# Half of the second thought's odd weight pairs split before it starts, the other half in its first step with slots of their own

## The chip, the cores and the metric

The kernel runs on one core of one Trainium2 chip. The metric is the device time of one execution in microseconds (us), the median of several runs. One execution is recorded by the hardware profiler, and all rows below are from that one.

## The reference

Two sequences of 2048 tokens with 1024 features, all in f32. The input goes through a half-weighted FFN block, a windowed attention and the same FFN block again. Of the FFN only the gate product and the "thought" need weights:

```python
x_norm = layer_norm(x, in_gamma, in_beta)
thought = x_norm[:, -1, :] @ agg_w + agg_b            # last token of each sequence, 1024 x 1024
for _ in range(K_STEPS):                              # 4 steps
    t = layer_norm(thought, pn_gamma, pn_beta)
    t = gelu(t @ d1_w + d1_b)                         # 1024 x 4096
    thought = thought + (t @ d2_w + d2_b)             # 4096 x 1024
broadcast = (thought @ bc_w + bc_b)[:, None, :]
gate = sigmoid(x @ gate_w + gate_b)
out = layer_norm(x + gate * broadcast, out_gamma, out_beta)
...
x = x + 0.5 * ffn(_layernorm(x))
x = x + attention(_layernorm(x))                      # windows of 128, squared relu, then @ w_o
x = x + 0.5 * ffn(_layernorm(x))
```

The thought is a chain of products for two rows (the last token of each sequence) whose 4 steps each go through all 32 MB of d1_w and d2_w.

## The kernel before

One program, PLAN, is a list of pieces in one order; each engine walks the list and issues what is its own of each piece, so the list sets the order on every engine's queue. TensorE (PE), VectorE (DVE), ScalarE (ACT), GpSimd (POOL) and SyncE (SP, which issues every DMA) meet by semaphores alone. The big products are f16 products of values split into a high and a low half (three products for one f32 product).

**Stages.** First come the folding of weights and the gate products of the 32 token tiles (to about 763 us). Stage 2 is the attention, in 16 groups of two tiles: per group `prep` pieces on DVE and ACT make the normalised tokens, a transposing DMA (`group_turn`, L989) brings them into the group's place, and PE makes q, v, score and collect from them. Stage 3 is the second FFN's gate products (from about 1734 us). The tokens of groups 0 and 1 lie in the slots 4 to 7 of `thought_units`; those of later groups in `gate_arena`.

**The thought** is computed twice (thought 0 beside stage 1, thought 1 beside stage 2), a few matmuls at a time between the pieces of the big work. `with_thought` hands them out as beats by a share of PE's time. A weight tile is 128 x 1024 f32, 512 KB; two of them make a pair, and a pair of tiles is used by 16 small matmuls in one go. d1 and d2 have 32 pairs together. A pair is used in one of these ways (`how`):

- `whole`: loaded as f32 and used as it is (L1258).
- `keep`: loaded as f32 (L851) into one of the slots for loads; `t_high` rounds it to f16 on ACT (L1469) into a slot for splits; `t_low` makes the rest on DVE (L1851); PE uses both halves from there (`t_unit`, L1268); SP stores the halves to `parts_scratch` (L945). So two tiles cost 2 loads, 2 ACT and 2 DVE instructions and 2 stores.
- `pair`: the stored halves are loaded back (L851, `thought_units<-parts_scratch`) and used (`t_pair`, L1268).

Thought 0 keeps the even pairs in its step 1. Thought 1 loads the even pairs back in its first step and keeps the odd ones there, all 16 of them, 32 tiles. From its second step on every pair is loaded back.

**Slots.** `thought_units` has 8 slots of a tile: 0 to 3 for loads (FOR_LOADS), 4 to 7 for splits (FOR_SPLITS). In thought 1's first step the loads of both kinds take turns in slots 0 to 3, so that in effect slots 3 and 0 hold the two tiles of a `pair` and slots 1 and 2 the raw tiles of a `keep`. From the second step on loads use all eight.

SP issues a slot's next load behind the piece that leaves the slot free, after waiting that it is free (`fetch_unit`, `await_left`). `t_high` waits for the raw tile and for a free split slot. Every one of these waits holds up all that stands behind it on its engine's queue.

## Time and profile before

| | us |
|---|---|
| median of 3 runs | 2074.18 |
| lowest and highest | 2071.38, 2074.87 |
| the profiled execution | 2078.41 |
| its span from first to last instruction | 2077.2 |
| TensorE busy | 1988.2 (96%) |
| VectorE busy | 1207.6 (58%) |
| ScalarE busy | 679.7 (33%) |
| GpSimd busy | 162.0 (8%) |

A difference from the time before counts only where TensorE is made to wait less or more, or to run at another clock. The rows that say where it waits are in the section after the next.

### The profile page before, as it was taken

The numbers are of one execution on the slowest core, as the hardware profiler recorded it, in microseconds if no ns is written. First come the engines' busy times: TensorE is split into PE (matmuls) and PEld (weight loads), VectorE is DVE, ScalarE is ACT, GpSimd is POOL, SyncE is SP. The second block draws the span as 40 slices with busy tenths as digits, with TensorE's granted clock in tenths as the row PEclk, the third lists the DMA queues.
The fourth block names the chain that finished last, engine by engine and source line by source line (L and its number), as shares of the span: only waits on it lengthen the run. The fifth ranks groups of instructions, "written<-read, shape, count | busy, mean of one in ns | idle before, by whom it ended". The sixth has DMA issues, their size and how long they took to land.

```text
span 2077.2 us, 30589 instructions
## 1 busy us (share of the span) xinstructions
PE 1988.2 (96%) x12010; PEld 1048.1 (50%) x12010; DVE 1207.6 (58%) x2152; ACT 679.7 (33%) x947; POOL 162.0 (8%) x278
## 2 busy tenths in 40 slices
PE   8999988999899899999999999999999999999997
PEld 3334433344343457655566655566656564444443
DVE  2323676223444465567666655655556536888887
ACT  0478545213223322223333212121112213444443
POOL 0000000000000010011001000000000001111111
PEclk9999998999999999999999999999999999999999
DMA  9599986879899743359989999798998947555552
GB/s 364 201 350 412 379 309 233 335 261 379 323 399 389 280 136 102 102 175 314 325 290 331 319 317 296 279 365 300 297 305 281 348 171 193 152 152 153 153 154 78
DMA packets 275214, 555.78 MB, mean 268 GB/s; under 512 B 149040, under 2 KB 149248, under 8 KB 274688
## 3 DMA queue, kind: packets, MB, share of 16 engines
q1 hardware_dynamic: 275072, 553.83, 76.6%
q8 instruction: 96, 1.57, 0.3%
q14 instruction: 46, 0.38, 0.0%
HBM read 406.93 MB, written 113.26 MB: 250 GB/s over the span
## 4 chain that ended last, share of the span: by engine, by line
PE 43%; DMA 4%; DVE 4%; SPq 2%; ACT 1%; issue 1%; POOL 0%; ACTq 0%; DVEq 0%
PE product_banks L1068 38%; PE product_banks L1203 2%; PE thought_acc L1268 2%; DMA thought_units<-parts_scratch 2%; DMA arena<-in_x 1%; SPq L989 1%; SPq L851 1%; DVE thought_units L1851 1%; DVE bn_parts L1492 0%; DMA gate_arena<-arena 0%; DMA arena<-x_scratch 0%; ACT arena L1384 0%; DVE arena L1663 0%; DVE arena L1639 0%; ACT arena L1387 0%
## 5 line engine op out<-in xcount | busy, mean ns | idle before, releaser
L1068 PE MATMUL product_banks<-gate_arena,arena 128*128 128x512 f16 x1536 | 355.5, 387 | 0.0
L1068 PE MATMUL product_banks<-wide_a,thought_units 128*128 128x512 f16 x1536 | 331.7, 379 | 0.8 <-DVE arena L1703 0.8
L1068 PE MATMUL product_banks<-gate_arena,wide_a 128*128 128x256 f16 x2688 | 301.6, 273 | 2.2 <-DMA gate_arena<-arena 2.2
L1068 PE MATMUL product_banks<-wide_b,gate_arena 128*128 128x512 f16 x1344 | 297.5, 379 | 0.0
L1068 PEld LDWEIGHTS product_banks<-gate_arena,wide_a 128*128 128x128 f16 x2688 | 261.6, 98 | 49.2 <-issue 19.3
L1068 PEld LDWEIGHTS product_banks<-gate_arena,arena 128*128 128x128 f16 x1536 | 150.6, 100 | 197.3 <-issue 40.4
L1068 PEld LDWEIGHTS product_banks<-wide_a,thought_units 128*128 128x128 f16 x1536 | 150.2, 98 | 182.6 <-DVE arena L1703 1.6
L1068 PEld LDWEIGHTS product_banks<-wide_b,gate_arena 128*128 128x128 f16 x1344 | 129.3, 98 | 160.8 <-issue 12.2
L1492 DVE BATCH_NORM_STATS2 bn_parts<-arena 128x6 f32<-128x512 f32 x256 | 164.2, 683 | 4.2
L1915 POOL TENSOR_TENSOR token_stats<-stats,minus_half 128x1 f32<-128x1 f32 x96 | 63.7, 664 | 1001.5 <-DVE stats L1500 848.4
L1672 DVE SCALAR_TENSOR_TENSOR gate_arena<-product_banks,gate_arena 128x256 f16<-128x256 f32 x128 | 54.1, 422 | 148.2 <-ACT gate_arena L1399 146.0
L1517 DVE SCALAR_TENSOR_TENSOR arena<-product_banks,inverse_gate,arena 128x512 f32<-128x512 f32 x64 | 47.9, 749 | 140.7 <-PE product_banks L1068 129.5
L1100 PE MATMUL product_banks<-wide_a,wide_b 128*128 128x512 f32 x256 | 120.8, 621 | 6.0 <-DMA wide_a<-in_w_attn 6.0
L1203 PE MATMUL product_banks<-arena,key_weights 128*128 128x512 f32 x248 | 114.3, 606 | 9.5 <-issue 5.3
L1915 POOL TENSOR_TENSOR stats<-stats,minus_half 128x1 f32<-128x1 f32 x64 | 68.1, 1063 | 705.0 <-DVE stats L1500 420.8
L1376 ACT ACTIVATE arena<-arena,token_stats 128x1024 f32<-128x1024 f32 x32 | 39.6, 1236 | 228.1 <-DMA arena<-in_x 228.0
L1405 ACT ACTIVATE arena<-product_banks,inverse_vo 128x512 f32<-128x512 f32 x64 | 43.8, 686 | 214.1 <-PE product_banks L1068 214.1
L1399 ACT ACTIVATE gate_arena<-product_banks 128x256 f16<-128x256 f32 x128 | 41.2, 379 | 199.8 <-PE product_banks L1068 199.8
L1268 PE MATMUL thought_acc<-thought_units,thought_parts 128*6 128x512 f16 x1344 | 96.8, 382 | 4.1 <-DMA thought_units<-parts_scratch 3.2
L1433 ACT ACTIVATE arena<-arena 128x512 f32<-128x512 f32 x64 | 40.3, 630 | 176.2 <-DVE arena L1517 176.2
L1663 DVE SCALAR_TENSOR_TENSOR arena<-arena 128x1024 f16<-128x1024 f32 x32 | 39.2, 1224 | 91.8 <-ACT arena L1387 91.8
L1100 PEld LDWEIGHTS product_banks<-wide_a,wide_b 128*128 128x128 f32 x256 | 48.5, 198 | 67.6 <-issue 67.5
(206 smaller groups left out, 2310.9 us busy)
## 6 DMA issues: line engine op xcount, KB each, us to landing
thought_units<-parts_scratch SPq DMA_DIRECT2D x272, 512.0 KB, 6.9
thought_units<-in_d_w SPq DMA_DIRECT2D x171, 512.0 KB, 7.5
arena<-in_x SPq DMA_DIRECT2D x64, 512.0 KB, 9.3
parts_scratch<-thought_units SPq DMA_DIRECT2D x64, 512.0 KB, 5.4
x_scratch<-arena SPq DMA_DIRECT2D x64, 512.0 KB, 8.2
thought_row<-in_d_w SPq DMA_DIRECT2D x53, 512.0 KB, 6.9
arena<-x_scratch SPq DMA_DIRECT2D x40, 512.0 KB, 7.5
gate_scratch<-arena SPq DMA_DIRECT2D x32, 512.0 KB, 8.0
```

The source lines that it names most:

```text
L1068: mm = pe.matmul(bank, left(i, k), right(j, k), start=(n == 0), stop=(n == 3 * KD - 1))
L1100: mm = pe.matmul(bank_ap(key), wide_b[:, e, d * P:(d + 1) * P], wide_a[:, e, h * BANK:(h + 1) * BANK], start=(e == 0), stop=(e == KD - 1))
L1203: mm = pe.matmul(bank_ap(key), weights_of(u)[:, side, :], value_slot(other)[:, h * BANK:(h + 1) * BANK], start=(side == 0), stop=(side == ...
L1268: mm = pe.matmul(thought_acc[at:at + PARTS * B, :], value, unit[:, part, h * BANK:(h + 1) * BANK], start=first and part == 0, stop=last an ...
L1376: act.activation(ph_slots[u % PREP_RING], px_slots[u % PREP_RING], ACT.Identity, bias=st[:, 1:2], scale=st[:, 0:1]).then_inc(h0_made, 1)
L1399: act.activation(queries[:, query_place(n * GROUP + i), 0, e - 1:e + 1, :], made[:, i], ACT.Copy, scale=QUERY_SCALE).then_inc(q_high_made, 1)
L1405: act.activation(value_slot(n * GROUP + i)[:, h * BANK:(h + 1) * BANK], bank_ap(key), ACT.Copy, scale=inverse["vo"][:, :]).then_inc(out_of ...
L1433: act.activation(res, res, ACT.Sigmoid).then_inc(gated_3, 1)
L1492: dve.bn_stats(bn_parts[:, h, :], source[:, h * BANK:(h + 1) * BANK]).then_inc(own.up(), 1)
L1517: dve.scalar_tensor_tensor(out=res[:, cols], in0=bank_ap(key), scalar=inverse["gate"][:, :], in1=bias[:, cols], op0=ALU.mult, op1=ALU.add) ...
L1672: low = dve.scalar_tensor_tensor(out=q[:, 1], in0=made[:, i], scalar=QUERY_SCALE, in1=q[:, 0], op0=ALU.mult, op1=ALU.subtract)
L1915: return pool.tensor_tensor(to, st[:, 2:3], minus_half[:, 0:1], ALU.pow)
```

## The change

16 of the 32 tiles that thought 1 kept in its first step (the pairs whose number is 1 modulo 4) are now loaded, rounded, split and stored between the two thoughts, from the last four gate tiles into group 2 of the attention. Slots 0 and 1 take their raw tiles, slots 2 and 3 the halves. In thought 1's first step these 8 pairs are loaded back as `pair`, so that the step has 24 pairs that are loaded back and 8 that are kept. The raw tiles of the kept ones get slots 6 and 7, their halves 4 and 5, and the `pair` tiles have all of 0 to 3. The first kept raw tiles wait for group 1's tokens to be used, their first halves for group 0's. Their `t_high` and `t_low` are placed only when a `t_unit` is one of the next two products of the thought. The wait of ACT for a score product is gone (it is now part of `await_left`).

```diff
     def use_of(self, owner):
 
         kind, n = owner
+        if kind == "tokens" or kind == "split" and self.splits[n].unit is None:
+            return "again"
...
         else:
-            slots = FOR_LOADS + (FOR_SPLITS if step else [])
+            slots = FOR_LOADS + FOR_SPLITS if step else FOR_SPLITS[GROUP:] if how == "keep" else FOR_LOADS
...
-        return "keep" if step == 0 and pair % 2 else "pair"
+        return "keep" if step == 0 and pair % 4 == 3 else "pair"
+
+    def split_between(self):
+
+        pairs = [("d1", [(k, c), (k, c + 1)]) for c in range(0, COLS_1, 2) for k in range(1, KD, 4)]
+        pairs += [("d2", [(k, 0), (k + 1, 0)]) for k in range(2, KH, 8)]
+        self.between = []
+        for matrix, pair in pairs:
+            made = []
+            for k, c in pair:
+                at = len(self.splits)
+                load = self.load(None, None, matrix, k, c, "keep", at, FOR_LOADS[:2])
+                slot = FOR_LOADS[2 + at % 2]
+                self.splits.append(Split(load, None, slot, self.take(slot, ("split", at))))
+                made.append(at)
+            for kind in ("high", "low"):
+                for at in made:
+                    self.between.append(self.step(None, (kind, at)))
...
-                        slot = FOR_SPLITS[at % len(FOR_SPLITS)]
+                        slot = FOR_SPLITS[at % (GROUP if tau else len(FOR_SPLITS))]
...
-            elif todo and i > first and s[0] in weights:
+            elif todo and i > first and s[0] in weights and (
+                    tau == 0 or any(x[0] == "unit" for x in [x for x in raw[i + 1:] if x[0] in weights][:2])):
...
-    out += paced([p for n in range(TILES - LATE, TILES) for p in plan_gate(n)], prep, 1.15, PE_PIECES)
-    out += [("sigmoid", TILES - 1, 1), ("gate_store", TILES - 1)]
-    out.append(("score_scale",))
-    out += plan_stage_2(0, B)
+    between = paced([p for n in range(TILES - LATE, TILES) for p in plan_gate(n)], prep, 1.15, PE_PIECES)
+    between += [("sigmoid", TILES - 1, 1), ("gate_store", TILES - 1)]
+    between.append(("score_scale",))
+    between += plan_stage_2(0, B)
+    out += paced(between, THOUGHTS.between, 0.38, PE_PIECES)
...
-        if kind == "split":
-            eng.wait_ge(unit_used, SPLITS[n].unit + 1)
+        if kind == "tokens":
+
+            eng.wait_ge(product_full, BANK_AT[("v", n, GROUP - 1, HALVES - 1)] + 1)
+        elif kind == "split":
+            if SPLITS[n].unit is not None:
+                eng.wait_ge(unit_used, SPLITS[n].unit + 1)
...
-                if n == STORE_2 or n == STORE_2 + GROUP:
-
-                    act.wait_ge(product_full, BANK_AT[("score", (n - STORE_2) // GROUP, 0)] + 1)
```

Line numbers shift by up to 38. **VectorE in the last gate tiles.** In the kernel before, L1626 is the first `prep` instruction of the attention's first tile (gate times thought), and the second L1492 of the piece belongs to the moments of the last gate tile:

```order
L1633 TENSOR_TENSOR arena<-arena,half_beta 128x1024
L1517 SCALAR_TENSOR_TENSOR arena<-product_banks,inverse_gate,arena 128x512 x2
L1626 TENSOR_TENSOR arena<-arena,thought_row 128x1024
L1509 SCALAR_TENSOR_TENSOR arena<-turn_banks,arena 128x512 x2
L1639 TENSOR_TENSOR arena<-arena 128x1024
L1492 BN_STATS bn_parts<-arena 128x6 x2
L1494 BN_AGGR stats<-bn_parts 128x2
L1500 TENSOR_SCALAR stats<-stats 128x1
L1492 BN_STATS bn_parts<-arena 128x6 x2
```

In the changed kernel L1886 is `t_low`, L1661 and L1527 are the two lines before:

```order
L1668 TENSOR_TENSOR arena<-arena,half_beta 128x1024
L1552 SCALAR_TENSOR_TENSOR arena<-product_banks,inverse_gate,arena 128x512 x2
L1886 SCALAR_TENSOR_TENSOR thought_units<-thought_units,unit_scale 128x1024
L1661 TENSOR_TENSOR arena<-arena,thought_row 128x1024
L1544 SCALAR_TENSOR_TENSOR arena<-turn_banks,arena 128x512 x2
L1674 TENSOR_TENSOR arena<-arena 128x1024
L1527 BN_STATS bn_parts<-arena 128x6 x2
L1529 BN_AGGR stats<-bn_parts 128x2
L1535 TENSOR_SCALAR stats<-stats 128x1
L1527 BN_STATS bn_parts<-arena 128x6 x2
```

One `t_low` now stands ahead of both.

**VectorE in group 1 of the attention.** Here nothing of the thought stood before. Now (L1683 to L1698 are `prep` of a tile, its last row ahead of the transposing DMA is L1698, and L1725 makes the weights that `collect` waits for):

```order
L1886 SCALAR_TENSOR_TENSOR thought_units<-thought_units,unit_scale 128x1024
L1668 TENSOR_TENSOR arena<-arena,half_beta 128x1024
L1674 TENSOR_TENSOR arena<-arena 128x1024
L1527 BN_STATS bn_parts<-arena 128x6 x2
L1529 BN_AGGR stats<-bn_parts 128x2
L1535 TENSOR_SCALAR stats<-stats 128x1
L1886 SCALAR_TENSOR_TENSOR thought_units<-thought_units,unit_scale 128x1024
L1683 SCALAR_TENSOR_TENSOR arena<-arena,stats,half_gamma 128x1024
L1688 SCALAR_TENSOR_TENSOR arena<-arena,stats 128x1024
```

Two `t_low` stand inside the chain of the group's second tile; a third stands ahead of the first tile's L1683.

**SyncE in thought 1's first step.** Before, for two neighbouring products of the thought (L945 stores halves, L972 to L976 fetch tokens, L995 and L1017 store tokens):

```order
L989 DMA_TRANSPOSE gate_arena<-arena 128x16x128
L851 DMA thought_units<-parts_scratch 128x1024 x2
L945 DMA parts_scratch<-thought_units 128x1024
L851 DMA thought_units<-in_d_w 128x1024
L945 DMA parts_scratch<-thought_units 128x1024
L851 DMA thought_units<-in_d_w 128x1024
L972 DMA arena<-in_x 128x1024
L976 DMA arena<-gate_scratch 128x1024
L972 DMA arena<-in_x 128x1024
L976 DMA arena<-gate_scratch 128x1024
L1017 DMA x_scratch<-arena 128x1024 x2
L851 DMA thought_units<-parts_scratch 128x1024 x2
```

Now (L983 stores halves, L889 loads, L1010 to L1055 are tokens):

```order
L889 DMA thought_units<-parts_scratch 128x1024 x4
L983 DMA parts_scratch<-thought_units 128x1024
L889 DMA thought_units<-in_d_w 128x1024
L983 DMA parts_scratch<-thought_units 128x1024
L889 DMA thought_units<-in_d_w 128x1024
L1010 DMA arena<-in_x 128x1024
L1014 DMA arena<-gate_scratch 128x1024
L1010 DMA arena<-in_x 128x1024
L1014 DMA arena<-gate_scratch 128x1024
L1055 DMA x_scratch<-arena 128x1024 x2
L889 DMA thought_units<-parts_scratch 128x1024 x6
```

Loads of stored halves come in fours and sixes, where they came in twos, and stores and raw loads are half as many.

## Rows read from the trace of the kernel before

**Rows 1.** Busy time of each engine by stretch; the first row is the columns.

```profile
core 0: us, PE busy (x) PEld busy (x) DVE busy (x) ACT busy (x) POOL busy (x), PEclk, DMA share, GB/s
718.00:918.00 200.00, 194.50 (x1279) 121.81 (x1278) 123.56 (x225) 52.77 (x76) 17.03 (x34) 1.00 0.40 126
918.00:1196.00 278.00, 266.52 (x1902) 168.22 (x1901) 194.58 (x356) 87.21 (x114) 24.86 (x46) 0.99 0.92 312
1196.00:1664.00 468.00, 462.13 (x3416) 281.97 (x3416) 270.94 (x552) 94.26 (x143) 32.22 (x78) 1.00 0.91 310
```

**Rows 2.** The same view in stretches of 52 us; PEclk is the granted clock.

```profile
936.00:988.00 52.00, 49.81 (x328) 28.42 (x326) 39.42 (x59) 20.53 (x26) 5.48 (x6) 0.97 0.98 314
988.00:1040.00 52.00, 49.74 (x368) 31.13 (x367) 34.44 (x58) 16.57 (x23) 4.05 (x10) 0.97 0.90 325
```

**Rows 3.** What TensorE waited for from 918 to 1196 us; total, times, longest.

```profile
PE product_banks L1203 <- issue: 3.3, 3, 2.0
PE thought_acc L1268 <- DMA thought_units<-parts_scratch: 2.5, 2, 2.3
PE product_banks L1068 <- DMA gate_arena<-arena: 2.2, 1, 2.2
PE thought_turn L1276 <- DVE t_wide L1858: 1.4, 1, 1.4
PE product_banks L1203 <- DVE key_weights L1690: 1.1, 1, 1.1
PE thought_acc L1268 <- DVE thought_units L1851: 0.9, 1, 0.9
```

**Rows 4.** Order of time, 960 to 1016 us: start, us, engine, line, idle before.

```profile
974.17 1.04 PE L1268 MATMUL thought_acc<-thought_units,thought_parts 128*6 128x512 f16 x16 [0.21 <-DMA thought_units<-parts_scratch]
...
992.58 1.51 SPq L851 DMA_DIRECT2D thought_units<-parts_scratch  x2
995.21 1.15 ACT L1469 ACTIVATE thought_units<-thought_units,unit_scale 128x1024 f16<-128x1024 f32 x1 [12.98 <-DMA thought_units<-in_d_w]
...
1007.78 1.79 PE L1268 MATMUL thought_acc<-thought_units,thought_parts 128*6 128x512 f16 x16 [2.26 <-DMA thought_units<-parts_scratch]
```

**Rows 5.** Instructions of L1469, 918 to 1196 us, and what they waited for.

```profile
L1469 ACT ACTIVATE thought_units<-thought_units,unit_scale x32: 1134/1148/1166, 918.6 to 1146.5; 128x1024 f16<-128x1024 f32 x32
...
  DMA thought_units<-in_d_w: 26.0, 8
```

**Rows 6.** Instructions of L1851, 918 to 1196 us.

```profile
L1851 DVE SCALAR_TENSOR_TENSOR thought_units<-thought_units,unit_scale x32: 1274/1280/1286, 927.4 to 1147.7; 128x1024 f16<-128x1024 f32 x32
```

**Rows 7.** What TensorE waited for from 718 to 918 us.

```profile
PE product_banks L1203 <- DVE key_weights L1690: 1.9, 1, 1.9
...
PE turn_banks L1077 <- ACT arena L1351: 0.5, 1, 0.5
```

**Rows 8.** ScalarE in order of time, 708 to 742 us: the tile's normalising.

```profile
739.87 1.24 ACT L1351 ACTIVATE arena<-arena,token_stats 128x1024 f32<-128x1024 f32 x1 [8.30 <-POOL token_stats L1922]
```

**Rows 9.** The transposing DMAs of L989, 740 to 870 us, issue to landing.

```profile
DMA to landing us min/median/max: 4.3/4.4/4.5
```

**Rows 10.** The same DMAs, 910 to 1196 us.

```profile
DMA to landing us min/median/max: 4.3/7.7/10.5
```

**Rows 11.** Order of time, 744 to 800 us: a transpose and its product.

```profile
762.55 1.91 SPq L989 DMA_TRANSPOSE thought_units<-arena  x1
...
773.17 21.12 PE L1068 MATMUL product_banks<-thought_units,wide_a 128*128 128x256 f16 x192
```

**Rows 12.** Order of time, 798 to 884 us: two more such pairs.

```profile
809.06 1.32 SPq L989 DMA_TRANSPOSE thought_units<-arena  x1
...
814.04 21.12 PE L1068 MATMUL product_banks<-thought_units,wide_a 128*128 128x256 f16 x192
...
855.47 1.93 SPq L989 DMA_TRANSPOSE gate_arena<-arena  x1
...
864.44 10.64 PE L1068 MATMUL product_banks<-gate_arena,wide_a 128*128 128x256 f16 x96
```

45 lines of the change are left out of this document (27 added, 18 removed).

## The prediction

> **What bounds the kernel now.** I read the busy time by stretch first: TensorE (PE) is the engine to look at, and what matters is not its busy time but what it lacks. From 718 to 918 us it lacks 200 - 194.5 = 5.5 us, from 918 to 1196 us 278 - 266.5 = 11.5 us, from 1196 to 1664 us 468 - 462.1 = 5.9 us [rows 1]. The second stretch is thought 1's first step, the third its other steps, the first is where the moved work goes. The step with the splits is thus the poorest: 4.1 us lacking in 100, against 1.3 in 100 later. The same view in short stretches shows that PE also had a lower clock there, 0.97 of full speed in two stretches of 52 us [rows 2], which is 2 x 0.03 x 52 = 3.1 us of work. So 11.5 + 3.1 = 14.6 us are to be had at most in this step. The waits of PE tell what they are: 3.3 and 1.1 us ahead of collect (L1203), 2.5 us for loads of stored halves, 2.2 us for a transposing DMA, 1.4 us for a copy of the sums, 0.9 us for a `t_low` [rows 3]. PE's own work stays the same: every pair still takes one run of 16 matmuls, whether from the splits or loaded back.
>
> **What goes away in the first step.** If it waited at the rate of the later steps, 5.9 / 468 x 278 = 3.5 us would remain [rows 1], so 14.6 - 3.5 = 11.1 us are owed to the splits and to what comes with them. I take it in two parts.
>
> (a) The loads of stored halves. One was issued at 992.6 us and PE began with its tiles at 1007.8 us, having waited 2.26 us; that run of 16 matmuls took 1.79 us where the one at 974 us took 1.04 [rows 4], so the clock had fallen behind the wait, to the lower of its two levels (1.2 instead of 2.4 GHz). With four slots in place of two such a load is issued one product of the thought earlier. The 2.5 us of [rows 3] and the lower clock of that stretch, 1.6 us [rows 2], should go: 4.1 us. (b) The rest of the 11.1 us, 7.0 us, are late collects, one late transposing DMA, a late `t_low`, and the other stretch at a lower clock. Behind them is the length of DVE's and ACT's queues. DVE runs 32 `t_low` of 1.28 us there [rows 6], 41 us of its 195 us [rows 1], and ACT's 32 `t_high` [rows 5] stood still for raw tiles 8 times, 26.0 us in all, once 12.98 us [rows 4, 5], with all else on ACT behind them. Halving the number halves these, 3.5 us; the raw tiles are now fetched two products ahead, so it may be more, up to the whole 7.0, or, if it is the attention's own chain that is late, nothing. I take 3.5. Sum: 4.1 + 3.5 = 7.6 us less, between 0 (nothing of it depends on the splits) and 11.1.
>
> The Trainium skill speaks for more than the first term: in "TensorE: Matmul & The Clock Gate", section "HAM oscillation — how this bites in real kernels", each wait of PE that throttles it is paid a second time in slow matmuls. The wait at 1007.8 us agrees (1.79 us for 1.04). Taken for every wait it would make the gain larger, and no row here shows that: of the 11.5 us of waits the clock's share is 3.1.
>
> **What comes between the thoughts.** 16 `t_high` of 1.15 us on ACT and 16 `t_low` of 1.28 us on DVE [rows 5, 6] go where ACT is busy 53 and DVE 124 of 200 us [rows 1]: 18 and 20.5 us, for which there is room on both. The loads and stores, 32 of 0.5 MB, are 17 MB in some 150 us, 112 GB/s on top of 126 GB/s, where 312 GB/s are moved later [rows 1]. So none becomes a bound. What costs is a `t_low` or a block of DMAs inside a chain that PE waits for. I find three such places.
>
> - The last gate tile. PE already waits 0.5 us there for the normalised tile [rows 7], which ACT makes at 739.9 us after a chain over DVE and POOL [rows 8]. A `t_low` stands in DVE's queue ahead of that chain, where DVE runs without a gap: 1.28 us more. It would be nothing if DVE had a gap, and I see none there; two more in the worst case 2.6.
> - Group 1's tokens. The second transposing DMA of group 1 is issued at 809.1 us and takes 4.4 us [rows 9], so it lands at 813.5; PE begins with them at 814.0 [rows 12]. The slack is 0.5 us, but it stands behind a wait for collect of 1.9 us [rows 7] that would take up part of a delay. Now a store and a load of 0.5 MB each are issued just ahead of it. With 4.4 us to landing as before it costs nothing; with the 7.7 us of the loaded stretch [rows 10] 3.3 - 0.5 = 2.8 us. I take 1.
> - Group 2's tokens. The DMA is issued at 855.5 us, lands at 859.9, and PE needs it at 864.4 [rows 12], slack 4.5 us. Three `t_low` in DVE's chain move it by 3 x 1.28 = 3.8 us: it fits by 0.7 us. With 7.7 us to landing it is late by 2.6. I take 1.
>
> For group 0's last tokens the DMA is issued at 762.6 us and PE comes at 773.2 [rows 11]: slack 10.6 - 4.4 = 6.2 us, against four `t_low` at most, 5.1 us. Nothing. The first kept raw tiles of thought 1 wait for group 1's value products, which lie before the collect that thought 1 has to wait for anyway. Nothing either. SP holds up the token DMAs behind a `t_low` by a microsecond or two, at places where their data are needed some 10 us later. Sum: 1.3 + 1 + 1 = 3.3 us more, between 0 and 8.
>
> **The sum.** -7.6 + 3.3 = -4.3 us. The profiled execution took 2078.4 us of which its span is 2077.2, and lies 4.2 us above the median; 2078.4 - 4.3 = 2074.1 there, 2074.2 - 4.3 = 2069.9 us for the median. Later steps of thought 1 have the same loads in a slightly different order, and stage 3 is untouched: both weigh nothing in the sum.
>
> **The rivals.**
>
> *Slower.* The transposing DMAs land later. They take 4.3 to 4.5 us in the quiet stretch [rows 9], and 7.7 (median) to 10.5 us [rows 10] where stores and loads of the thought go beside them; the change brings such stores and loads into the quiet stretch. At 7.7 us the prices are 1.3 at the gate tile, 5.1 + 3.3 - 6.2 = 2.2 for group 0, 2.8 and 2.6 us for groups 1 and 2: 8.9 us, and if the clock falls behind three of the waits as in [rows 4], 0.75 us in a run and as much again in the next, 1.5 us each, 4.5 more. If of the first step only (a) is won, 4.1 us, this gives 13.4 - 4.1 = 9.3 us slower, 2083.5 us; with the full 7.6 us won 2080.0. I take 2080. It decides from about 5.5 us to landing on. Against it: the traffic stays under what the loaded stretch has, 238 against 312 GB/s. Chance 0.14. The Trainium skill has the mechanism ("DMA: Bandwidth & Descriptors", "Queues, rings and completion order"): all that SP issues goes through one row of rings, and each engine consumes the descriptors in ring order, so a transpose stands behind the store and load issued ahead of it. With the same page's some 358 GB/s for a core, two tiles ahead would be an estimated 2.9 us; the rows' own difference is 3.3 us.
>
> *The waits only move.* The waits in the first step come from how the pieces of attention and thought happen to meet, each 1 to 2 us and none of them twice at the same place. Then a new order of beats makes new ones at the rate of before, and only (a) and a little of (b) is won, say 5, while 3.3 are paid: 2072.5 us. For it: half of the splits still stand there, the step gets denser (its first to last product in less time), and DMA is 0.92 busy in the step [rows 1], so that even with more slots a load may come late. Chance 0.30.
>
> *More is won.* If ACT's standing still for raw tiles is what makes the collects and the transposing DMA late, all of (b) goes: -11.1 + 3.3 = -7.8, and with 1.3 alone paid between -9.8: 2065.5 us. Chance 0.14.
>
> *It does not do what it says* can be left out: the rows of the order show the splits moved and the number of stores halved in the step.
>
> **How the numbers follow.** The forecast of 2069.9 us has 0.42, from 2067 to 2072.5. The range of 8 in 10 reaches from 2063.5 to 2078.5: it takes in the larger gain, the moved waits, and a third of the slower case. A difference of 0.2% is 4.15 us, about what a measurement of this kernel can tell from no change, so faster means under 2070.0 us. That is the case in 0.14 of the larger gain, about 0.25 of the 0.42 of the forecast, and 0.06 of the moved waits: 0.45. Slower means over 2078.3: 0.12 of the first rival and 0.02 of others: 0.14. The same: 0.41.
>
> **What would show it.** In the changed kernel's busy time by stretch PE should lack about 11.5 - 5.5 = 6 us in the first step, and the granted clock should be 1.00 in all but perhaps one stretch; the waits for `parts_scratch` in it should be under 0.5 us; ACT's waits for raw tiles (L1504 there) under 10 us. From 718 to 918 us PE should lack about 5.5 + 3.3 = 9 us, with 1.8 us at the last gate tile. The transposing DMAs there should take 4.4 to 5.5 us. Wrong would be: over 12 us lacking between the thoughts, or the first step at 10 us still, with collects waiting for DVE as before.

## The result, and the profile after

| | before | after |
|---|---|---|
| time, us (median, range, runs) | 2074.52 (2071.38 to 2077.39, 4) | 2102.51 (2100.13 to 2103.86, 4) |
| ratio to before | | 1.0123, interval 1.0103 to 1.0143 |
| span of the profiled execution, us | 2077.2 | 2101.5 |
| granted clock over the span | 0.986 | 0.981 |

The change makes the kernel 1.2% slower: 25.5 us (21 to 30) by the ratio, 28 by the medians. The forecast was 4.3 us faster, and its range ended at 2078.5.

Where the time went is told by the same piece of work in both traces. What stood at 718 us before stands at 720 now, what stood at 918 at 933, 1196 at 1217, 1664 at 1688. So 13 us were lost between the thoughts, 6 in the first step of thought 1, 3 in its later steps. Stage 3 keeps the distance. The 2 us at 718 are older than the change: up to there the kernels run all but the same program, and the single profiles of all the kernels below lie between 4 us ahead of before and 3 us behind it at that place. The cuts follow the attention's pieces; the thought's own first step ends inside the second stretch, at 1156 us before and at 1148 now (the copy of its last sums, L1858 and L1893). First the busy time by stretch, cut at these places (before: [rows 1]):

```profile
core 0: us, PE busy (x) PEld busy (x) DVE busy (x) ACT busy (x) POOL busy (x), PEclk, DMA share, GB/s
720.00:933.00 213.00, 196.89 (x1286) 122.94 (x1284) 142.72 (x243) 69.44 (x92) 19.79 (x34) 0.98 0.63 205
933.00:1217.00 284.00, 269.39 (x1944) 169.13 (x1941) 172.16 (x334) 70.00 (x98) 21.15 (x46) 0.98 0.85 290
```

Between the thoughts TensorE lacks 213 - 196.9 = 16.1 us (5.5 before), at a clock of 0.98. In the first step it lacks 284 - 269.4 = 14.6 (11.5 before), at 0.98 as well (0.99 before). What it waited for in the first step (columns: total, times, longest; before: [rows 3]):

```profile
PE thought_acc L1306 <- DMA thought_units<-parts_scratch: 12.0, 4, 6.5
PE thought_turn L1276 <- DVE thought L1926: 2.1, 1, 2.1
PE product_banks L1106 <- DMA gate_arena<-arena: 0.5, 1, 0.5
```

All that stood in the rows of before but the loads is nearly gone: late collects, the late transposing DMA, the copy of the sums and the late `t_low` made 8.9 us of waits, and now 2.6 are left. The loads of stored halves made 2.5 us, and now make 12.0. ScalarE's 16 `t_high` of the step waited 0.7 us for raw tiles, where 32 had waited 26.0 [rows 5]:

```profile
L1504 ACT ACTIVATE thought_units<-thought_units,unit_scale x16: 1132/1145/1151, 947.1 to 1121.5; 128x1024 f16<-128x1024 f32 x16
...
  DMA thought_units<-in_d_w: 0.7, 1
```

The longest of the load waits, TensorE in order of time (start, duration, ..., times; in brackets the idle time before it):

```profile
1065.27 1.04 PE L1306 MATMUL thought_acc<-thought_units,thought_parts 128*6 128x512 f16 x16
...
1074.21 0.60 PE L1306 MATMUL thought_acc<-thought_units,thought_parts 128*6 128x512 f16 x8
1081.34 1.02 PE L1306 MATMUL thought_acc<-thought_units,thought_parts 128*6 128x512 f16 x8 [6.53 <-DMA thought_units<-parts_scratch]
```

A beat with two pairs ran at 1065.3 us, the next one began at 1074.2 and stood still in its middle for 6.53 us. SyncE's queue around it, and the time from issue to landing of the two loads (L889) that are issued at 1065.9 and 1066.3 us:

```profile
1060.35 1.09 SPq L1010 DMA_DIRECT2D arena<-in_x  x1
...
1063.66 0.99 SPq L1055 DMA_DIRECT2D x_scratch<-arena  x2
```

```profile
L889 SPq DMA_DIRECT2D thought_units<-parts_scratch x2: 320/391/462, 1065.9 to 1066.3; - x2
...
DMA to landing us min/median/max: 14.0/14.4/14.9
```

They were issued as soon as the first beat had freed its slots, and landed 14.0 and 14.9 us later. Ahead of them stand ten transfers of 0.5 MB that SyncE had issued from 1058.2 us on and that were still on their way: two stores of halves, two raw tiles, four token fetches (two each of L1010 and L1014) and two token stores. Meanwhile the DMA engines moved 417 GB/s, more than the 290 of the whole step:

```profile
1066.00:1081.00 15.00, 8.81 (x88) 7.06 (x80) 6.60 (x12) 4.51 (x7) 0.27 (x2) 0.88 1.03 417
```

At that rate a transfer of 0.5 MB takes 1.26 us, and the ten with the two loads themselves are twelve, an estimated 15.1 us: the landing time is that of a queue. The beats are 8.9 us apart. In the front part and in the prediction a count has to be put right here: a pair takes 8 matmuls, and the run of 16 is a beat of two pairs. It matters for the slots, below.

What TensorE waited for between the thoughts (before: [rows 7]):

```profile
PE product_banks L1241 <- DVE key_weights L1725: 6.1, 1, 6.1
PE product_banks L1106 <- DVE gate_arena L1707: 3.6, 1, 3.6
PE thought_turn L1270 <- DMA t_wide<-arena: 3.2, 1, 3.2
PE turn_banks L1115 <- ACT arena L1389: 1.6, 1, 1.6
```

The wait for the last gate tile is 1.6 us, where 1.8 was expected. The large ones were not: 3.6 us for the rounded queries of a product (L1707 on VectorE) and 6.1 us for the scores' weights (L1725), ahead of group 0's first collect; and 3.2 us for the rows with which thought 1 begins (`t_wide`), which SyncE now fetches at 882.0 us, behind the last stores of halves, and fetched at 865.9 us before.

### The profile page after: what moved, and what is told of

Same layout as the page of the kernel before. It is cut to its first block and busy times, and to the rows that moved or that the text cites. A ratio compares the mean times of both kernels' runs of the same rounds, so it can differ in the third digit from the quotient of the medians.

```text
span 2101.5 us, 30604 instructions
## 1 busy us (share of the span) xinstructions
PE 1992.9 (95%) x12010; PEld 1050.0 (50%) x12010; DVE 1207.6 (57%) x2152; ACT 679.1 (32%) x947; POOL 161.1 (8%) x278
## 5 line engine op out<-in xcount | busy, mean ns | idle before, releaser
L1527 DVE BATCH_NORM_STATS2 bn_parts<-arena 128x6 f32<-128x512 f32 x256 | 164.3, 684 | 4.4
L1707 DVE SCALAR_TENSOR_TENSOR gate_arena<-product_banks,gate_arena 128x256 f16<-128x256 f32 x128 | 54.1, 422 | 146.7 <-ACT gate_arena L1437 144.4
L1698 DVE SCALAR_TENSOR_TENSOR arena<-arena 128x1024 f16<-128x1024 f32 x32 | 39.2, 1224 | 109.0 <-ACT arena L1425 109.0
```

Of the source, the lines that this page charges most:

```text
L1527: dve.bn_stats(bn_parts[:, h, :], source[:, h * BANK:(h + 1) * BANK]).then_inc(own.up(), 1)
L1707: low = dve.scalar_tensor_tensor(out=q[:, 1], in0=made[:, i], scalar=QUERY_SCALE, in1=q[:, 0], op0=ALU.mult, op1=ALU.subtract)
```

## The experiments

Each kernel was timed against the kernel before. "Behind" is (ratio - 1) x 2077 us, with its interval. Single executions of one kernel differ by some us (2070 to 2080 in e6), so where one profile is read, differences under 3 us are not made use of. The distance between two kernels of the table is uncertain by 4 to 7 us, by their two intervals. e2, e3, e5, e6, e7b, e9, e10b and e17 use wrong weights or factors in place of what they leave out, and tell of time alone.

| kernel | ratio | interval | us behind before |
|---|---|---|---|
| the changed kernel | 1.0123 | 1.0103 to 1.0143 | 25.5 |
| e1 between alone | 1.0074 | 1.0052 to 1.0096 | 15.4 |
| e2 first step alone | 1.0018 | 1.0004 to 1.0032 | 3.7 |
| e3 no loads between | 1.0093 | 1.0073 to 1.0114 | 19.3 |
| e4 high, low in turn | 1.0079 | 1.0061 to 1.0097 | 16.4 |
| e5 first step all loaded, 8 slots | 0.9927 | 0.9911 to 0.9942 | -15.2 |
| e6 first step all loaded, 4 slots | 0.9987 | 0.9975 to 0.9999 | -2.7 |
| e7b no work between | 1.0047 | 1.0035 to 1.0060 | 9.8 |
| e8 clear of the scores | 1.0108 | 1.0093 to 1.0122 | 22.4 |
| e9 two more slots | 1.0034 | 1.0016 to 1.0052 | 7.1 |
| e10b VectorE's work alone | 1.0098 | 1.0077 to 1.0120 | 20.4 |
| e11 beats 3 us later | 1.0081 | 1.0057 to 1.0106 | 16.8 |
| e12 in VectorE's gaps | 1.0121 | 1.0098 to 1.0145 | 25.1 |
| e13 the same, raw tiles earlier | 1.0062 | 1.0044 to 1.0080 | 12.9 |
| e14 e13 and beats later | 1.0072 | 1.0057 to 1.0088 | 15.0 |
| e15 before, beats later | 1.0009 | 0.9994 to 1.0023 | 1.9 |
| e16 e13, last rounding behind the values | 1.0086 | 1.0064 to 1.0109 | 17.9 |
| e17 e16 and two more slots | 0.9999 | 0.9985 to 1.0013 | -0.2 |

### The two halves of the change apart

e1 keeps the sixteen splits between the thoughts and has the first step of before (the diffs here and below are against the changed kernel where nothing else is said):

```diff
-        return "keep" if step == 0 and pair % 4 == 3 else "pair"
+        return "keep" if step == 0 and pair % 2 else "pair"
...
-            slots = FOR_LOADS + FOR_SPLITS if step else FOR_SPLITS[GROUP:] if how == "keep" else FOR_LOADS
+            slots = FOR_LOADS + (FOR_SPLITS if step else [])
...
-                        slot = FOR_SPLITS[at % (GROUP if tau else len(FOR_SPLITS))]
+                        slot = FOR_SPLITS[at % len(FOR_SPLITS)]
...
```

> The kernel before with the sixteen extra splits between the thoughts and nothing else of the change: the eight pairs are rounded and stored there, and then once more in the first step as before, so the first step is that of before and the extra stored copies are read by nobody. Theory of the queue (the traces of before and after side by side): the loads, roundings and stores between the thoughts stand ahead of token fetches and transposing DMAs on SP's queue and ahead of the token tiles' instructions on ACT, which costs 13.6 us between 718 and 893 us; this kernel then takes 2074.5 + 13.6 = 2088 us (2084 to 2092). The prediction's own step (3.3 us between the thoughts) would give 2078. If it is 2074, the loss between the thoughts comes from somewhere else.

e2 leaves out all that stands between the thoughts:

```diff
-        self.split_between()
+        self.between = []
...
+for n, load in enumerate(LOADS):
+    if load.how == "pair" and (load.matrix, load.k, load.c) not in STORE_OF:
+        STORE_OF[load.matrix, load.k, load.c] = STORE_OF[load.matrix, load.k - (1 if load.matrix == "d1" else 2), load.c]
```

> The kernel after without anything between the thoughts: in the first step of the second thought, and in the later ones, the eight pairs that would have been stored between the thoughts load the stored halves of the pair before them (k-1, or k-2 in d2), so their products are computed from the wrong weights, with the same number of loads, matmuls and slots as in the changed kernel. The prediction's step (7.6 us won in the first step) gives 2067. Theory of the slots (the stored halves still come into four slots that a beat uses up two at a time, and there are half again as many of them): the first step loses 6 to 8 us by itself, 2081 (2078 to 2084). Rival, that the first step of the changed kernel only suffers from what happened between the thoughts: 2074 or less.

Measured: 15.4 us behind for e1 (10.8 to 20), 3.7 for e2 (0.8 to 6.6). The sum is 19.1, and 6.4 us of the changed kernel's 25.5 come only with both together; by the intervals that rest may also be nothing. The profiles speak for nothing: at 718 us, ahead of all that was changed, the changed kernel's stood 2.1 us behind before, e1's 0.6 and e2's 1.3 ahead, and counted from there their spans are 22.2, 14.8 and 6.4 us longer, which leaves 1.0. What e1 waited for between the thoughts, and then what e2 waited for in the first step:

```profile
PE product_banks L1240 <- DVE key_weights L1724: 3.4, 1, 3.4
PE product_banks L1105 <- DVE gate_arena L1706: 3.3, 1, 3.3
PE thought_turn L1269 <- DMA t_wide<-arena: 3.2, 1, 3.2
```

```profile
PE thought_acc L1310 <- DMA thought_units<-parts_scratch: 9.6, 4, 6.5
```

So most of the loss is made where the prediction had 3.3 us, and the first step wins nothing by itself where it had 7.6. The theory written before these runs was right on e1 and 3 us too dark on e2.

### What the price between the thoughts is made of

e3 takes the raw tiles away, e7b the work (it keeps loads, waits and stores), e10b ACT's part of the work.

```diff
-                load = self.load(None, None, matrix, k, c, "keep", at, FOR_LOADS[:2])
+                load = len(self.loads)
+                self.loads.append(Load(matrix, k, c, "resident", at, FOR_FIRST[at % 2], 0, None))
...
```

> The changed kernel with the sixteen roundings and stores between the thoughts, but without their sixteen loads of raw tiles: both halves are made from a tile that is already in the chip (the first thought's row), so the stored halves are wrong and ACT waits for no load there, and SP issues no load there; ScalarE's and VectorE's work and the stores stay. Theory of the queue: ACT's waits for the raw tiles (25.8 us in six waits) and SP's loads are what holds up the token tiles, so 9 to 12 of the 13.6 us go: 2092 (2089 to 2095). Rival, that the rounding work itself (16 x 1.15 us on ACT, 16 on DVE) and the stores cost it: 2100 to 2103.

```diff
...
+                to, of = parts_at(split.slot)[:, 0], unit_at(load.slot)
+                if split.unit is None:
+                    to, of = to[:, 0:8], of[:, 0:8]
+                act.activation(to, of, ACT.Copy,
...
+                if split.unit is None:
+                    low, raw, high = low[:, 0:8], raw[:, 0:8], high[:, 0:8]
...
```

> The changed kernel with its loads, waits and stores between the thoughts, but the roundings there done on 8 columns of 1024, which takes their work from ACT and DVE (the stored halves are wrong, and in the second thought the pairs concerned load the pair before instead). With the loads taken away the loss between the thoughts stayed at 10.5 of some 13 us. If the work is what costs, above all a rounding's second half on VectorE ahead of the scores' weights (collect waited 6.1 us), 7 to 10 us go here: 15 to 18 us behind the kernel before. If it is the waits and the queue that cost, nothing goes: 25 us behind.

```diff
...
+                if split.unit is None:
+                    to, of = to[:, 0:8], of[:, 0:8]
+                act.activation(to, of, ACT.Copy,
...
+                                         in1=parts_at(split.slot)[:, 0] if split.unit is not None else half_gamma[:, :],
```

> The changed kernel with ACT's half of the roundings between the thoughts done on 8 columns, and VectorE's half at full length (reading gamma instead of the first half; the stored halves are wrong, and the second thought loads the pair before instead). With both halves' work gone the kernel was 9.8 us behind before, with both there 25.5. If VectorE carries the price (it is busy 128 us of the 191 there, ACT 65), this stays at 22 to 25 us behind; if ACT's 18 us do, about 10; if each does a part, 15 to 18.

Measured: 19.3 us behind without the loads, 9.8 without the work, 20.4 with VectorE's work alone. Both theories of mine had a part wrong. The loads, which I held for the cause, are 6 us of it. The work is 15.7, more than I gave it, of which VectorE's 16 instructions of 1.28 us account for 10.6 and ACT's 16 of 1.15 for the other 5.1. The 6 and the 5.1 are no larger than what two such times can differ by; the 15.7 and the 10.6 are clear of it. Loads, work and the 3.7 of e2 add up to 25.6 of the 25.5. Both engines had been idle for a third of the stretch and more. Without the work TensorE waits between the thoughts as before (1.9 us for the weights), but for 1.9 us for the row of the thought:

```profile
PE product_banks L1246 <- DVE key_weights L1733: 1.9, 1, 1.9
PE thought_turn L1275 <- DMA t_wide<-arena: 1.9, 1, 1.9
```

How so little work costs so much is to be seen in the changed kernel's queues. VectorE ahead of the collect, in order of time:

```profile
815.03 0.29 DVE L1725 SCALAR_TENSOR_TENSOR key_weights<-key_weights 128x128 f32<-128x128 f32 x1
815.24 1.28 DVE L1886 SCALAR_TENSOR_TENSOR thought_units<-thought_units,unit_scale 128x1024 f16<-128x1024 f32 x1
818.94 1.23 DVE L1698 SCALAR_TENSOR_TENSOR arena<-arena 128x1024 f16<-128x1024 f32 x1 [2.43 <-ACT arena L1425]
820.09 0.34 DVE L1721 SCALAR_TENSOR_TENSOR key_weights<-product_banks,score_scale,keep_prev 128x128 f32<-128x128 f32 x1
```

Behind the first weights (815.03) come a `t_low` (L1886) and the `prep_low` of group 1's second tile (L1698), which waits for ACT, and only then the other weights (820.09). TensorE has been idle since 815.6:

```profile
806.25 4.12 PE L1106 MATMUL product_banks<-gate_arena,thought_units 128*128 128x128 f16 x48 [3.62 <-DVE gate_arena L1707]
...
821.68 5.29 PE L1241 MATMUL product_banks<-arena,key_weights 128*128 128x512 f32 x8 [6.12 <-DVE key_weights L1725]
```

In the kernel before it came to the same collect at 810.54, having waited 1.92 us:

```profile
810.54 3.67 PE L1203 MATMUL product_banks<-arena,key_weights 128*128 128x512 f32 x8 [1.92 <-DVE key_weights L1690]
```

The two rows of the collect also show the clock: its 8 matmuls took 5.29 us, where before 8 took 3.67, and over their first 3.6 us the granted clock was 0.55 (before 1.00). The wait of 6.1 us is paid again in part. That agrees with the Trainium skill, "TensorE: Matmul & The Clock Gate", section "HAM oscillation — how this bites in real kernels", which the prediction had cited and then counted only for waits of 2 us.

And why is VectorE late? Its token tiles are. SyncE's queue of the changed kernel, from the transposing DMA of group 0's second tile to group 1's first fetch (L1010):

```profile
771.22 2.06 SPq L1027 DMA_TRANSPOSE thought_units<-arena  x1
773.34 0.85 SPq L960 DMA_DIRECT2D gate_scratch<-arena  x1
774.24 0.44 SPq L983 DMA_DIRECT2D parts_scratch<-thought_units  x1
774.72 0.91 SPq L889 DMA_DIRECT2D thought_units<-in_d_w  x1
775.68 1.19 SPq L960 DMA_DIRECT2D gate_scratch<-arena  x1
776.98 0.40 SPq L1010 DMA_DIRECT2D arena<-in_x  x1
```

The fetch is issued at 776.98 us. Before, it was at 766.11:

```profile
766.11 0.85 SPq L972 DMA_DIRECT2D arena<-in_x  x1
```

Ahead of it in the queue stand two gate stores, a store of halves and a raw tile; the last two are new and account for 2.2 of the 10.9 us. The other 8.7 are those of the transposing DMA of group 0's second tile, which is issued at 771.2 us instead of 762.6 [rows 11]. VectorE and ScalarE ahead of it:

```profile
759.76 1.28 DVE L1886 SCALAR_TENSOR_TENSOR thought_units<-thought_units,unit_scale 128x1024 f16<-128x1024 f32 x1
760.96 1.28 DVE L1683 SCALAR_TENSOR_TENSOR arena<-arena,stats,half_gamma 128x1024 f32<-128x1024 f32 x1
...
762.31 1.15 ACT L1504 ACTIVATE thought_units<-thought_units,unit_scale 128x1024 f16<-128x1024 f32 x1 [4.69 <-DMA thought_units<-in_d_w]
766.19 0.63 ACT L1402 ACTIVATE arena<-arena 128x512 f32<-128x512 f32 x1 [2.73 <-DVE arena L1552]
```

And the tile's instruction (L1683 now, L1648 then) in the kernel before:

```profile
753.17 1.31 DVE L1648 SCALAR_TENSOR_TENSOR arena<-arena,stats,half_gamma 128x1024 f32<-128x1024 f32 x1
```

It starts 7.8 us later. Two of these are the older lateness of this profile; the others are four `t_low` (at 732.2, 740.5, 753.9 and 759.8 us) and a `t_high` (749.9), which stand one behind the other in the chain that leads to this tile, and move it by 1.1 to 1.3 us each. The long wait of ScalarE for a raw tile (4.69 us, until 762.31) cost nothing here: ScalarE stood idle behind it again until VectorE had made its next input, at 766.19.

So each queue in turn holds up the next: VectorE and ScalarE the token tile behind roundings, SyncE the next group's fetches behind that tile's transposing DMA, VectorE the weights behind that group's tiles. VectorE begins the first tile of group 1 at 785.3 us instead of 773.1, 12.2 us later, while TensorE, beside whose products for group 0 these tiles are made, begins them 3.2 us later (776.3 instead of 773.2 [rows 11]). So VectorE has 9 us less for the two tiles, with further `t_low` among their instructions. The experiments agree: the same fetch is issued at 770.7 us in e7b, without the work, and at 772.6 in e3, without the raw tiles.

### Can the order cure it?

e4 sets first and second halves in turn, e8 also keeps them from the stretch before the collect.

```diff
-            for kind in ("high", "low"):
-                for at in made:
+            for at in made:
+                for kind in ("high", "low"):
                     self.between.append(self.step(None, (kind, at)))
```

> The changed kernel with one edit: between the thoughts the pieces come as high, low, high, low instead of high, high, low, low, so that three pieces instead of two lie between the fetch of a raw tile and the rounding that waits for it, and a rounding's second half follows its first one piece later. Theory of the queue: ACT's waits for raw tiles shrink, and with them a third to a half of the 13.6 us: 2097 (2094 to 2100). Rival, that the roundings' work counts and not the waits: 2102.

```diff
-    out += paced(between, THOUGHTS.between, 0.38, PE_PIECES)
+    clear, other, due = (between.index(("q", 0, 3)), between.index(("collect", 0, 1))), list(THOUGHTS.between), 0.0
+    for i, piece in enumerate(between):
+        out.append(piece)
+        if piece[0] in PE_PIECES and not clear[0] <= i <= clear[1]:
+            due += 0.47
...
```

> The kernel with high, low, high, low between the thoughts (16.4 us behind the kernel before) with one more edit: no rounding stands between the fourth product of group 0 (q 0 3) and its first collect, where two second halves of 1.28 us stood on VectorE ahead of the scores' weights; the others come a little closer together (0.47 a piece instead of 0.38). If VectorE's order there is what makes the collect wait (6.15 us, against 1.92 before) and what lowers the clock behind it (0.89 in 800:830), 4 to 6 us go: 10 to 12 us behind the kernel before. If the wait comes from the token tiles' late start instead, nothing goes: 16.

Measured: e4 16.4 us behind, 9 less than the changed kernel, more than I had expected from it. e8 22.4: my reason for it fell. The wait for the weights became 5.2 us instead of 6.15, since the fetches of group 1 were still 6 us late, and a new one of 7.1 us came ahead of thought 1, whose row is fetched by SyncE behind the last store of the splits, which the edit had moved there.

e12, with the halves in turn as in e4, sets each piece by hand into a place where VectorE was idle in the trace of before, and group 1's fetches ahead of the stores.

```diff
...
+PLACES = [("gate", 28, 0, 0), ("gate", 28, 0, 2), ("gate", 28, 1, 0), ("gate", 28, 1, 2),
+          ("gate_store", 31), ("prep_fetch", 1), ("gate_store", 31), ("prep_fetch", 1),
+          ("q", 0, 1), ("q", 0, 4), ("score", 0, 0, 2), ("v", 0, 1, 1, 1), ("v", 0, 1, 1, 2), ("collect", 0, 1),
+          ("q", 1, 0), ("q", 1, 2), ("q", 1, 3), ("q", 1, 4), ("q", 1, 5), ("q", 1, 6), ("q", 1, 7), ("v", 1, 0, 0, 1),
+          ("v", 1, 1, 0, 1), ("score", 1, 1, 2), ("score", 1, 0, 0), ("score", 1, 0, 2),
+          ("v", 1, 1, 1, 0), ("v", 1, 1, 1, 1), ("v", 1, 1, 1, 1), ("v", 1, 1, 1, 2), ("v", 1, 1, 1, 2), ("collect", 1, 0)]
...
```

> The changed kernel with its sixteen roundings between the thoughts set by hand into the places where the trace of before shows VectorE idle (9.2 us while group 1's tokens come, 2 to 6 us around the collects and the q products of group 1), high and low in turn, group 1's token fetches ahead of the stores, and none in the last three gate tiles. If the price is that VectorE's and ACT's work stands ahead of the token tiles, most of it goes: collect's wait returns to 2 to 3 us (6.1), and the kernel is 8 to 12 us behind before instead of 25.5. If the sum of work counts wherever it stands: 16 or more.

Measured: 25.1 us behind, nothing won. TensorE's waits between the thoughts tell why:

```profile
PE product_banks L1258 <- ACT arena L1460: 12.1, 1, 12.1
...
PE product_banks L1258 <- DVE key_weights L1742: 1.9, 1, 1.9
```

Group 0's collect waited 1.9 us, as before: that far the places were right. Group 1's collect waited 12.1 us for values that ACT copies (L1460). SyncE, and ACT, around it:

```profile
862.71 1.94 SPq L1044 DMA_TRANSPOSE gate_arena<-arena  x1
...
865.74 0.44 SPq L906 DMA_DIRECT2D thought_units<-in_d_w  x1
```

```profile
872.36 1.15 ACT L1521 ACTIVATE thought_units<-thought_units,unit_scale 128x1024 f16<-128x1024 f32 x1 [7.67 <-DMA thought_units<-in_d_w]
873.41 0.67 ACT L1460 ACTIVATE arena<-product_banks,inverse_vo 128x512 f32<-128x512 f32 x1
```

The raw tile that was fetched at 865.74 us, behind a transposing DMA and a store, is the one for which ACT's rounding waited 7.67 us, until 872.36; the values stood behind that rounding. Work ahead of the tokens had been exchanged for a wait at the head of a queue. e13 fetches each raw tile earlier, by one more rounding in the gate tiles (its diff is against e12); e16 sets the last rounding behind the values (against e13).

```diff
-          ("gate_store", 31), ("prep_fetch", 1), ("gate_store", 31), ("prep_fetch", 1),
+          ("gate", 29, 0, 1), ("gate", 29, 0, 2), ("gate_store", 31), ("prep_fetch", 1),
+          ("gate_store", 31), ("prep_fetch", 1), ("q", 0, 1), ("q", 0, 4), ("score", 0, 0, 2), ("v", 0, 1, 1, 1),
...
```

> As the kernel whose roundings stand in VectorE's idle places, with one of them more in the gate tiles (behind gate 29 0 2), and by that every later one a place earlier, so that the fetch of each raw tile is issued 8 us or more ahead of its rounding. In the kernel before it group 0's collect waited 1.92 us, as before, but group 1's waited 12.1 us, because on ACT the rescaled values of that group stood behind a rounding that waited 7.7 us for its raw tile. Theory of the order (what counts is which token instruction stands behind a rounding or behind a load that a rounding waits for): that wait returns to 1.1 us and the kernel is 25.1 - 11 = 14 us behind before (11 to 17). Theory of the amount (64 us of DMA, 18 of ACT and 20 of VectorE cost their price wherever they stand): 20 to 25 us, with waits elsewhere.

```diff
-          ("v", 1, 1, 1, 0), ("v", 1, 1, 1, 2)]
+          ("v", 1, 1, 1, 2), ("collect", 1, 0)]
```

> As the kernel with the raw tiles earlier (12.9 us behind before), with one rounding moved: the last one's first half stands behind the values of group 1 on ACT (behind v 1 1 1 2) instead of ahead of them, where it waited for its raw tile and group 1's collect waited 5.2 us for it. Theory of the order: the collect waits 1.1 us as before, and with the lower clock behind it 4 to 6 us go: 7 to 9 us behind before. Theory of the amount: the wait turns up elsewhere, 11 or more.

Measured: 12.9 us behind (9 to 17) for e13 and 17.9 (13 to 23) for e16. TensorE's waits between the thoughts, of e13 and then of e16:

```profile
PE product_banks L1259 <- ACT arena L1461: 5.2, 1, 5.2
```

```profile
PE product_banks L1259 <- DVE key_weights L1743: 5.2, 2, 3.3
PE thought_turn L1288 <- DMA t_wide<-arena: 3.0, 1, 3.0
```

e13 came where the theory of the order had it: half of the 25.5 us depended on what stood behind what. e16 did not: the wait for the values went, and one for the weights (3.3 us) and one for the thought's row (3.0) came in its place; by their intervals its time can't be told from e13's. So the order explains about half, and I found none that makes the 16 splits free in these 175 us.

### The first step: slots

e5 and e6 load every pair of the first step back, and round nothing in thought 1 or between the thoughts. They differ in the slots alone: e5, whose diff this is, has eight and e6 four.

```diff
...
-        return "keep" if step == 0 and pair % 4 == 3 else "pair"
+        return "pair"
...
-            slots = FOR_LOADS + FOR_SPLITS if step else FOR_SPLITS[GROUP:] if how == "keep" else FOR_LOADS
+            slots = FOR_LOADS if matrix == "agg" else FOR_LOADS + FOR_SPLITS
...
```

> Nothing between the thoughts, and no rounding in the second thought at all: in its first step every pair loads stored halves, into eight slots as in the later steps (the pairs that no one stored load the halves of the pair before them, so their products are computed from wrong weights). This is the end to which the change goes a part of the way. If the rounding in the first step (64 us of ACT and DVE, 16 pairs) is what TensorE lacks there, all 14.6 us of lack and low clock of the first step shrink to the 3.5 of a later stretch of that length: 11 us faster than before. If the loads are the bound (twice as many as in the changed kernel's pairs that are loaded), it is no faster than before, within 3 us.

> As the one with eight slots, but the stored halves of the first step come into four slots, as in the changed kernel. Theory of the slots: a beat uses up two pairs, so with four slots their successors are fetched only one beat ahead (landing 3 to 15 us after issue, beats 5 to 16 us apart), and TensorE waits for them: 8 us or more behind the kernel with eight slots. Rival, that four slots are enough and the changed kernel's first step loses to its bursts of stores and raw loads: within 3 us of the eight slots.

Measured: 15.2 us faster than before with eight slots (12 to 18), 2.7 with four. First e5's stretch of the first step, in which TensorE lacks 1.5 us at full clock, then e6's wait for loads there:

```profile
918.00:1196.00 278.00, 276.49 (x2050) 175.03 (x2048) 164.83 (x343) 54.42 (x86) 19.60 (x47) 1.00 0.87 293
```

```profile
PE thought_acc L1310 <- DMA thought_units<-parts_scratch: 6.5, 6, 2.5
```

The idea of the change is thus right: with no rounding in the step the kernel can be 15 us faster, and 10 of them are what TensorE no longer lacks in the step (1.5 us for 11.5). But four slots take 12.5 of the 15 away again. e9 tries the same in the changed kernel, whose loads get the two slots of the first thought's row; the gates are multiplied by another vector in its place:

```diff
...
-            slots = FOR_LOADS + FOR_SPLITS if step else FOR_SPLITS[GROUP:] if how == "keep" else FOR_LOADS
+            slots = FOR_LOADS + FOR_SPLITS if step else FOR_SPLITS[GROUP:] if how == "keep" else FOR_LOADS if matrix == "agg" else FOR_LOADS + FOR_FIRST
...
-                dve.tensor_tensor(gb, gb, thought_row[:, GROUP_OF[u // GROUP][0], :], ALU.mult).then_inc(gate_spread, 1)
+                dve.tensor_tensor(gb, gb, half_gamma[:, :], ALU.mult).then_inc(gate_spread, 1)
```

> The changed kernel whose stored halves in the first step of the second thought come into six slots instead of four: the two slots under the first thought's row are taken for them, and the token tiles' gates of stage 2 are multiplied by gamma instead of that row (a wrong factor of the same size, the same instructions). With nothing rounded in the first step, eight slots against four were worth 12.4 us. Theory of the slots: TensorE's waits for stored halves in the first step (12.0 us in four waits) fall below 4, and the kernel gains 6 to 9 us on the changed one: 17 to 20 us behind before instead of 25.5. Rival, that the waits come from where single bursts of transfers happen to fall (6.5 us of them are one wait): less than 3 us gained.

Measured: 7.1 us behind, 18.4 less than the changed kernel. The first step by stretch and waits:

```profile
928.00:1200.00 272.00, 270.27 (x2002) 172.99 (x2000) 177.67 (x348) 69.64 (x98) 20.29 (x47) 1.00 0.88 306
```

```profile
PE thought_turn L1281 <- DVE thought L1931: 1.7, 1, 1.7
```

No wait for a load is left. The 12.0 us of waits and the clock, 0.98 to 1.00 over 284 us or 5.7 us, are together 17.7 of the 18.4; by the collects in both traces the work of those 284 us takes 266 in e9 (929 to 1195 us). Against e1, which has the same work between the thoughts and the first step of before, e9 is 15.4 - 7.1 = 8.3 us shorter (2 to 14): with six slots the changed first step is worth about what the prediction gave it with four, 7.6.

### Where the beats fall

Two long waits of the changed kernel hang on which piece a beat falls behind (the 6.5 us for a load, and 4.0 us at 1581.6 us for a copy of the sums that stands on VectorE behind a token instruction). e11 moves all beats of thought 1; e14 does so in e13, and e15 in the kernel before.

```diff
-def with_thought(main, beats):
+def with_thought(main, beats, due=0.0):
...
-    out += with_thought(plan_stage_2(B, GROUPS - 1), THOUGHTS.beats[1])
+    out += with_thought(plan_stage_2(B, GROUPS - 1), THOUGHTS.beats[1], -3.0)
```

> The changed kernel with every beat of the second thought set 3 us later among the main work, nothing else. Theory of accident: two of its longest waits in the second thought (6.5 us for stored halves whose loads were issued behind four token fetches and two stores, 4.0 us for the copy of the sums behind a token instruction that waits for its tile) hang on which piece a beat falls behind; moved by 3 us they vanish or change by 3 us or more in sum, so the time moves by 3 to 8 us, more likely down. Theory that these are the price of four slots and of the share of work: the same time within 2 us, with waits of like sum elsewhere.

> As the one with the raw tiles earlier, and with the second thought's beats 3 us later as well. In the changed kernel that shift alone took the time from 25.5 us behind before to 16.8. If the two causes add up (the order between the thoughts; where the beats of the second thought fall), this is 14 - 8 = 6 us behind before (2 to 10), and still not faster, since the first step keeps four slots. If the shift only bought back what the loss between the thoughts had displaced, it brings nothing here: 12 to 16 us behind.

> The kernel before with the second thought's beats 3 us later, nothing else: a control. If where the beats fall is a matter of accident of some 5 us in either kernel, this differs from before by 3 to 8 us in either direction. If only the changed kernel, with four slots for half again as many stored halves, depends on it, this is the time before within 2 us.

Measured: 16.8 us behind for e11, 8.7 less than the changed kernel; but 15.0 for e14, 2.1 more than e13, and 1.9 for e15, which can't be told from before. So the shift is no cure, and it doesn't add up with the order. In the profile of e11 the same two places did change (3.6 us of wait for the load instead of 6.5, and 7.4 for loads in all instead of 12.0; none at the sums), others came (3.8 us for other sums, 4.4 for squares). Why it won 8.7 us (2 to 15) in one kernel and nothing in the next I leave open.

### Both together

> That kernel with six instead of four slots for the stored halves of the first step (the token tiles' gates of stage 2 multiplied by gamma instead of the first thought's row, as in the earlier kernel with two more slots). There the slots took 18.5 us off the changed kernel. If order and slots are the two causes of the loss and add up, this is 8 - 18 = some 10 us faster than before (2062 to 2072 where before is 2077): the change's idea pays once both are cured. If part of the 18.5 us only made up for the loss between the thoughts (at 1130 us that kernel stood 3.8 us ahead of before, having been 11.5 behind at 870), the gain is 0 to 4 us.

e17 is e16 with the edit of e9. Measured: 0.9999, the time of before. Slots were worth 18.4 us in the changed kernel and 18.1 here, so they act for themselves, whatever is lost between the thoughts. The 10 us of gain that I expected did not come, because e16 itself had stayed at 17.9. No kernel that computes the reference's result beat the kernel before in these runs; e5, with wrong weights, shows what there would be to win.

## Why the prediction was wrong

Two terms of the sum failed, (a) with its sign and the price between the thoughts with its size. The signs of being wrong that it had named came: TensorE lacks 16.1 us between the thoughts, where over 12 was named, and 14.6 in the first step, where 10 was, though not with collects that wait.

**(a), the loads: 4.1 us less.** Wrong in sign, and the step that failed is a sentence: "with four slots in place of two such a load is issued one product of the thought earlier". A beat uses up two pairs, so of the three pairs that two beats load back, two reuse slots that were freed only one beat before; the third is fetched two beats ahead. There are half again as many such loads, and they come between stores and fetches. Their waits went from 2.5 to 12.0 us and the clock stayed low (0.98). e6, e5 and e9 show it: without more slots the loads wait (6.5 us in e6), with them they don't.

**(b), the splits: 3.5 us less.** Right in kind and too small. The waits other than loads fell from 8.9 to 2.6 us, ACT's waits for raw tiles from 26.0 to 0.7 (under 10 had been named as the sign). The bound "up to the whole 7.0" was the better value.

**Between the thoughts: 3.3 us more.** It was 15.4 (e1). The bound of 8 did not hold either. Three things failed. "SP holds up the token DMAs behind a `t_low` by a microsecond or two" was 10.9 us at group 1's fetches (776.98 against 766.11), and 7.7 when the 3.2 by which TensorE was late there are taken off. The price was set up place by place, each with its own slack, and for group 0's last tokens it came out at nothing since TensorE comes for them 10.6 us later; but the same DMA stands on SyncE ahead of group 1's fetches, and who waits for those was not asked. And apart from the gate tile I looked for places where TensorE waits for a transposing DMA; 9.7 us of waits came from VectorE's order ahead of the queries and the scores' weights, and 3.2 from SyncE's ahead of thought 1's first rows. "There is room on both" engines was true of the busy time and decided nothing: VectorE's 20 us of work, on an engine idle for a third of the time, cost half that on the path (10.6, e10b against e7b).

**The single places.** The last gate tile: 1.6 us for 1.8, right. Group 1's and group 2's tokens: no wait, where 1 us had been taken for each. The transposing DMAs landed in 4.3 to 5.6 us (4.4 to 5.5 named), so the "slower" rival had its sign right and its mechanism wrong: it decided from landing times that never came.

**The later steps weigh nothing in the sum.** They lost 3 us, of which the wait at the sums is visible; e2 has it too. It is where beats fall once the light pieces are fewer.

**The rival that waits only move** had been given to the first step alone. There the waits of the collects did not move but went, and longer ones for loads came, for which the slots are the cause. It fits between the thoughts instead: e12 and e16 show waits that moved on when their place was cleared.

**The range** reached 8.6 us above the forecast and the result lies 32.6 above it. It summed slacks of single places; none of its cases held a chain through three queues, nor loads that wait longer than before.

## What to carry to other kernels

When work is moved into a stretch that looks idle, follow every in-order queue it enters (the DMA queue too) and ask of each instruction behind it who waits for that one in turn, over two or three steps; the busy share does not tell the price. Count slots against what one use frees at once: with four slots, all freed by one use, most loads were issued no earlier than with two, and here two more were worth 18 us, more than all the moved work could win (15). Split such a change into its halves on the chip first: the half that was to win was bounded by e5 in one run.

## What the runs showed of the hardware

A load's time to landing was 3.1 us at the least and 14.9 at the most within one step, at the same size of 0.5 MB, by what had been issued ahead of it; the longest is that of twelve transfers at the measured 417 GB/s.

One order of work can show a wait of two sizes without a difference in time. e9 has the same order between the thoughts as the changed kernel; its product with the queries and its collect:

```profile
802.18 6.92 PE L1111 MATMUL product_banks<-gate_arena,thought_units 128*128 128x128 f16 x48 [3.45 <-DVE gate_arena L1712]
...
817.60 5.37 PE L1246 MATMUL product_banks<-arena,key_weights 128*128 128x512 f32 x8 [3.33 <-DVE key_weights L1730]
```

Behind a wait of 3.45 us the 48 matmuls took 6.92 us, at a granted clock of 0.57; in the changed kernel, behind a wait of 3.62 us, they took 4.12 at 1.00. The collect begins 15.4 us after them in both (817.60 - 802.18 and 821.68 - 806.25), since VectorE's weights decide when. So the wait ahead of it is 3.33 us in one and 6.12 in the other, and nothing is won by the shorter. In e1 it is 3.38, behind 48 matmuls of 6.86 us. Why waits of like length were followed by the lower clock in one run and not in the other is not shown.
